# The first expert network in pairs of tiles, with four pairs in flight and a shorter inverse root

## The reference

```python
x = x + _L0_gnn_ref(_layernorm(x), ...)   # per relation sums of edges, block-diagonal weights
x = x + _L0_ffn_ref(_layernorm(x)[None], ...)[0]   # the part that the change touches
x = x + _L1_gnn_ref(_layernorm(x), ...)   # attention over edges
x = x + _L1_ffn_ref(_layernorm(x)[None], ...)[0]   # eight gated networks per row
```

```python
h = jax.nn.gelu(jnp.einsum('nd,edf->enf', xf, W1) + b1[:, None, :], approximate=False)
y = jnp.einsum('enf,efd->end', h, W2) + b2[:, None, :]
out = jnp.einsum('ne,end->nd', w_dense, y).reshape(B, S, D)
out = _layer_norm(out + x, gamma, beta)
```

## Time and profile before

| | |
|---|---|
| runs shown | 4926.8, 4935.69, 4936.24 us, median 4935.69 us |
| profiled execution | 4932.26 us, span 4930.4 us |
| mean granted TensorE clock | 0.842 of full speed |
| busy, share of the span | PE 84%, weight loads 66%, DVE 41%, ACT 18%, POOL 63% |
| `ffn0`, first hidden matmul to the end of the last row | 2176.84 to 2697.30 us |

### The profile page before, as it was taken

One profiled execution on the slowest core, in us unless ns is written; L12 is line 12 of the kernel. 1 busy time (PEld: TensorE's weight loads), 2 busy tenths in 40 slices (PEclk: granted clock), 3 DMA queues, 4 the chain that ended last, 5 costly groups with the idle time before them and its releaser, 6 DMA issues. The chain is left out here.

```text
span 4930.4 us, 66111 instructions
## 1 busy us (share of the span) xinstructions
PE 4146.8 (84%) x18994; PEld 3241.6 (66%) x18994; DVE 2022.2 (41%) x8072; ACT 895.6 (18%) x1880; POOL 3130.4 (63%) x3273
## 2 busy tenths in 40 slices
PE   2888878877788778858886689999999999999998
PEld 2777777877778778745564346666666666666665
DVE  5455555555555555524443223323332333233321
ACT  3111111111111111123332011111111111111112
POOL 3777777777777777710000677777777777777750
PEclk6667677777766776679997689999999999999999
DMA  5344444444444444411111544444444444444430
GB/s 166 113 122 121 122 122 121 121 122 123 121 121 121 121 121 123 121 56 40 46 39 33 157 118 118 123 126 123 118 123 127 122 118 127 128 123 117 127 94 10
DMA packets 270659, 544.10 MB, mean 110 GB/s; under 512 B 62129, under 2 KB 165825, under 8 KB 270482
## 3 DMA queue, kind: packets, MB, share of 16 engines
q0 software_dynamic: 155584, 431.06, 31.7%
q1 hardware_dynamic: 71890, 70.98, 4.6%
q10 hardware_dynamic: 43008, 40.36, 2.5%
HBM read 482.17 MB, written 59.99 MB: 110 GB/s over the span
## 5 line engine op out<-in xcount | busy, mean ns | idle before, releaser
L1560 POOL DMA_INDIRECT ring<-table,index x1616 | 1553.2, 961 | 548.6 <-issue 491.9
L651 POOL DMA_INDIRECT ring<-xn,index x1612 | 1528.9, 948 | 565.1 <-issue 477.3
L766 PE MATMUL bank<-spare,ring 128*128 128x64 f32 x6448 | 1063.7, 337 | 426.0 <-DMA ring<-xn,index 392.2
L766 PEld LDWEIGHTS bank<-spare,ring 128*128 128x128 f32 x6448 | 1027.2, 251 | 452.9 <-issue 398.8
L1731 PE MATMUL bank<-ring,acc 128*128 128x264 f32 x3232 | 884.4, 411 | 118.2 <-DMA ring<-table,index 112.1
L1731 PEld LDWEIGHTS bank<-ring,acc 128*128 128x128 f32 x3232 | 599.6, 196 | 424.5 <-DMA ring<-table,index 241.3
L1909 DVE TENSOR_SCALAR acc<-iota,off 128x128 f32<-128x128 f32 x1734 | 355.6, 298 | 636.3 <-ACT off L1573 633.3
L865 DVE TENSOR_TENSOR cells<-cells,bank 128x128 f32 x812 | 233.9, 288 | 427.5 <-PE bank L766 345.2
L845 DVE TENSOR_SCALAR spare<-iota,scal 128x64 f32<-128x64 f32 x1612 | 407.2, 337 | 0.0
L1747 PE MATMUL bank<-acc,wa 128*128 (+1 forms) x832 | 381.4, 601 | 26.7 <-ACT ework L1608 26.7
L1772 PE MATMUL bank<-wo,ework 128*128 128x256 f32 x1664 | 381.6, 383 | 1.8 <-DVE y L1980 1.8
(11 more groups left out here) (268 smaller groups left out, 3281.3 us busy)
## 6 DMA issues: line engine op xcount, KB each, us to landing
ring<-table,index POOLq DMA_INDIRECT x1616, 2.8
ring<-xn,index POOLq DMA_INDIRECT x1612, 2.8
sums<-acc ACTq DMA_DIRECT2D x101, 132.0 KB, 2.0
sums<-spare ACTq DMA_DIRECT2D x101, 128.0 KB
acc<-sums ACTq DMA_DIRECT2D x13, 528.0 KB
y<-x SPq DMA_DIRECT2D x13, 512.0 KB
table<-frow SPq DMA_DIRECT2D x48, 132.0 KB, 1.7
nsums<-sums ACTq DMA_DIRECT2D x49, 128.0 KB
```

Of the source, the lines that this page charges most:

```text
L651: pool.indirect_dma_start(ring[:, m * BT + t, :], None, k.xn_d, bass.IndirectOffsetOnAxis(ap=index[m][:, t:t + 1], axis=0)).then_inc(got[m ...
L766: ins = pe.matmul(win[q][:, t, h * CELLS:(h + 1) * CELLS], ring[:, m * BT + q * QUAD + t, h * P:(h + 1) * P], onehot[:, q * QUAD + t, :], ...
L1560: pool.indirect_dma_start(ring[:, par * BT + t, :], None, k.table1_d, bass.IndirectOffsetOnAxis(ap=index[par][:, t:t + 1], axis=0)).then_i ...
```

## The change

`ffn0` is written anew. The unit is a pair of tiles: 25 pairs, the last with one tile of 128 rows. `pair_steps` runs step s on every engine, and in step s there is work of four pairs: the hidden layer of pair s, the output of pair s-1 (both chunk by chunk, in turn), the norms and the turn of pair s-2, and the projection and the rows of pair s-3. There are four banks for the hidden chunks in place of two. PE's identity matmuls, ACT's `xg` and ACT's copy of y go away; in their place POOL makes `res`, x1 times its inverse deviation plus b2 (two instructions), beside the one that adds beta, and DVE adds `res` as it reads the bank (`add`). `gnn0` keeps the inverse deviations with one more DVE copy per tile. `inverse_root` is 11 instructions in place of 14. The first hidden matmul no longer waits for the load of `wp`.

```diff
@@ -160,13 +160,12 @@
     st.then(dve.tensor_scalar(t.bitcast(I32), x.bitcast(I32), 1, None, ALU.arith_shift_right))
     st.then(dve.tensor_scalar(guess.bitcast(I32), t.bitcast(I32), -1.0, float(0x5f3759df), ALU.mult, ALU.add))
     for _ in range(3):
-        st.then(dve.tensor_tensor(t, guess, guess, ALU.mult))
+        st.then(dve.scalar_tensor_tensor(t, guess, -0.5, guess, ALU.mult, ALU.mult))
         st.then(dve.tensor_tensor(t, t, x, ALU.mult))
-        st.then(dve.tensor_scalar(t, t, -0.5, 1.5, ALU.mult, ALU.add))
-        st.then(dve.tensor_tensor(guess, guess, t, ALU.mult))
-INVERSE_ROOT_STEPS = 14
+        st.then(dve.scalar_tensor_tensor(guess, t, 1.5, guess, ALU.add, ALU.mult))
+INVERSE_ROOT_STEPS = 11
 
 
 def past_waits(eng, k):
@@ -865,7 +864,7 @@
                     dve.tensor_tensor(here, here, win[q][:, u, :].rearrange("p (c n) -> p c n", n=NEAR), ALU.add
                                       ).then_inc(added if u == QUAD - 1 else chain, 1)
 
-            NORMS = 5 + INVERSE_ROOT_STEPS
+            NORMS = 6 + INVERSE_ROOT_STEPS
 
             def norm(j, par, loaded):
                 st = Steps(dve, steps, NORMS * j, k)
@@ -880,6 +879,7 @@
                 st.then(dve.bn_aggr(mv[:], stats[:]))
                 st.then(dve.tensor_scalar(var[:], mv[:, 1:2], LN_EPS, None, ALU.add))
                 inverse_root(dve, st, var[:], rstd[:], tmp[:])
+                st.done(dve.tensor_copy(k.rstd1[:, cols(j, 1)], rstd[:]))
                 if not (isinstance(j, int) and j == 0):
...
+def group_norm_steps(n):
+    return 2 * n + 1 + INVERSE_ROOT_STEPS
+PAIR = 2
+PCOLS = PAIR * P
+PAIRS = -(-NODE_TILES // PAIR)
...
+def pair_steps(eng, step):
+    first, last = 4, PAIRS - 3
+    assert first % 2 == 0 and last % 2 == 0
+    for s in range(first):
+        step(s, s % 2, s // 2)
+    with eng.Fori(first // 2, last // 2) as i:
+        step(2 * i, 0, i)
+        step(2 * i + 1, 1, i)
+    for s in range(last, PAIRS + 3):
+        step(s, s % 2, s // 2)
...
+    BANKS = 4
...
+        hid = a.sb("hid", [P, 2, C, PCOLS])
+        x1, res, x1b, x2 = (a.sb(f"f{n}", [P, 2, PAIR, D]) for n in ("x1", "res", "x1b", "x2"))
+        y, xn2 = (a.sb(f"f{n}", [P, PAIR, D]) for n in ("y", "xn2"))
...
+            def load(i, par):
+                if not (isinstance(i, int) and i < 2):
+                    sp.wait_ge(x1b_made, i - 1)
+                sp.dma_start(x1[:, par, 0:tiles_of_pair(i), :], rows_of(k.x1_all, 0, i)).then_inc(x_load[par], 16)
+            def store_x2(i, par):
+                sp.wait_ge(x2_done, i + 1)
+                sp.dma_start(rows_of(k.x2_all, AHEAD - AHEAD0, i), x2[:, par, 0:tiles_of_pair(i), :]
+                             ).then_inc(x2_stored[par], 16)
+            def store_row(i, t):
+                sp.wait_ge(row_done, PAIR * i + t + 1)
+                skip = AHEAD0 if isinstance(i, int) and i == 0 and t == 0 else 0
+                sp.dma_start(k.table1_d[cols(PCOLS * i + P * t + skip - AHEAD0, P - skip), :], row[skip:P, t, :]
+                             ).then_inc(row_stored[t], 16)
+            def step(s, par, half):
+                if is_pair(s + 1):
+                    load(s + 1, 1 - par)
+                if is_pair(s - 2):
+                    store_x2(s - 2, par)
+                if is_pair(s - 3):
+                    for t in range(tiles_of_pair(s - 3)):
+                        store_row(s - 3, t)
+            load(0, 0)
+            sp.dma_start(wp[:, :, 0:D], g["L1_gnn_W"].rearrange("(h p) d -> p h d", p=P)).then_inc(w_load, 16)
+            pair_steps(sp, step)
+            for par in range(2):
+                sp.wait_ge(x2_stored[par], 16 * len(range(par, PAIRS, 2)))
...
+            def residual(i, par, half):
+                n = tiles_of_pair(i)
+                here = res[:, par, 0:n, :]
+                pool.wait_ge(x_load[par], 16 * half + 16)
+                if not (isinstance(i, int) and i < 2):
+                    pool.wait_ge(y_added, PAIR * i - PAIR)
+                pool.tensor_tensor(here, x1[:, par, 0:n, :], k.rstd1[:, cols(PAIR * i, n)].unsqueeze(2).broadcast_to(
+                    [P, n, D]), ALU.mult).then_inc(res_step, 1)
+                pool.wait_ge(res_step, i + 1)
+                pool.tensor_tensor(here, here, each(b2[:], n), ALU.add).then_inc(res_made, 1)
+            def add_beta(i, par):
+                n = tiles_of_pair(i)
+                if not (isinstance(i, int) and i < 2):
+                    pool.wait_ge(x2_done, i - 1)
+                pool.tensor_tensor(x1b[:, par, 0:n, :], x1[:, par, 0:n, :], each(beta[:], n), ALU.add
+                                   ).then_inc(x1b_made, 1)
+            def step(s, par, half):
+                if is_pair(s):
+                    residual(s, par, half)
+                if is_pair(s - 1):
+                    add_beta(s - 1, 1 - par)
+            pool.wait_ge(small, 32)
+            pool.wait_ge(b2_kept, 1)
...
-                for h in range(H):
-                    pe.matmul(yb[:r, h * P:(h + 1) * P], xg[:, h, t * P:t * P + r], k.ident[:],
-                              start=(h == 0), stop=False, skip_group_check=True)
...
+            def hidden(i, par, c):
+                n = P * tiles_of_pair(i)
+                if not (isinstance(i, int) and i == 0 and c < BANKS):
+                    pe.wait_ge(h_kept, C * i + c - BANKS + 1)
+                for h in range(H):
+                    ins = pe.matmul(h_ps[c % BANKS][:, :n], k.w1[:, c // (C // 2), h, c % (C // 2) * P:(c % (C // 2) + 1) * P],
+                                    k.acc[:, h, cols(PCOLS * i, n)], start=(h == 0), stop=(h == H - 1))
+                ins.then_inc(h_made, 1)
+            def output(i, par, u):
+                t, first = u // (C // PAIR), u % (C // PAIR) * PAIR
+                if t >= tiles_of_pair(i):
+                    return
+                if first == 0:
+                    if not (isinstance(i, int) and i == 0):
+                        pe.wait_ge(y_added, PAIR * i - PAIR + t + 1)
+                    if t == 0:
+                        pe.wait_ge(h_kept, C * i + C)
+                for c in range(first, first + PAIR):
+                    ins = pe.matmul(y_ps[t], hid[:, par, c, t * P:(t + 1) * P], k.w2[:, c // (C // 2), c % (C // 2), :],
+                                    start=(c == 0), stop=(c == C - 1))
+                if first == C - PAIR:
+                    ins.then_inc(y_made, 1)
+            def turn(i):
+                pe.wait_ge(normed, i + 1)
+                if not (isinstance(i, int) and i == 0):
+                    pe.wait_ge(t_kept, i)
+                for t in range(tiles_of_pair(i)):
+                    for h in range(H):
+                        ins = pe.transpose(t_ps[:, h * PAIR + t, :], xn2[:, t, h * P:(h + 1) * P], k.ident[:])
+                ins.then_inc(turned, 1)
+            def project(i, t):
+                if isinstance(i, int) and i == 0 and t == 0:
+                    pe.wait_ge(wp_made, 1)
+                    pe.wait_ge(b2_kept, 1)
+                if t == 0:
+                    pe.wait_ge(t_kept, i + 1)
+                if not (isinstance(i, int) and i == 0 and t == 0):
+                    pe.wait_ge(p_moved, PAIR * i + t)
+                for h in range(H):
+                    ins = pe.matmul(p_ps, xt[:, h, t, :], wp[:, h, :], start=(h == 0), stop=(h == H - 1))
+                ins.then_inc(p_made, 1)
+            def step(s, par, half):
                 for c in range(C):
+                    if is_pair(s):
+                        hidden(s, par, c)
+                    if is_pair(s - 1):
+                        output(s - 1, 1 - par, c)
+                    if is_pair(s - 3) and c in (1, 4) and c // 4 < tiles_of_pair(s - 3):
+                        project(s - 3, c // 4)
+                if is_pair(s - 2):
+                    turn(s - 2)
+            pe.matmul(p_ps[:, 0:D], k.ones[0:1, :], k.b2[0:1, :], start=True, stop=True).then_inc(b2_made, 1)
+            pair_steps(pe, step)
...
-                act.copy(y[:r, t, :], y_ps[t % 2][:r, 0:D]).then_inc(y_moved, 1)
...
+            def keep(i, par, c):
+                n = P * tiles_of_pair(i)
+                act.wait_ge(h_made, C * i + c + 1)
+                act.activation(hid[:, par, c, :n], h_ps[c % BANKS][:, :n], ACT.Gelu,
+                               bias=k.b1[:, c // (C // 2), c % (C // 2):c % (C // 2) + 1]).then_inc(h_kept, 1)
...
+            def grow(i, t):
+                act.wait_ge(p_made, PAIR * i + t + 1)
+                act.activation(grown[:, t, :], p_ps[:, D:ROW1], ACT.Exp, scale=k.fm[:, 0:1],
+                               bias=k.fm[:, 1:2]).then_inc(grown_made, 1)
+            def step(s, par, half):
+                for c in range(C):
+                    if is_pair(s):
+                        keep(s, par, c)
+                    if is_pair(s - 3) and c in (1, 4) and c // 4 < tiles_of_pair(s - 3):
+                        grow(s - 3, c // 4)
```

(17 more changed lines are left out.)

## The result

The changed kernel takes 4975.2 us (median of 4 runs, 4966.0 to 4985.5), the kernel before 4931.5 us (4 runs, 4926.8 to 4936.2). The ratio is 1.0092, with a 95% interval of 1.0073 to 1.0111: slower by 44 us. The forecast was 4908 us, range 4874 to 4940, with 0.75 on faster and 0.10 on slower. It was wrong in sign, and the time lies outside the range.

A forecast was written before the change was run, and what follows sets the result against it. The prediction took a loop of waits in `ffn0`, through PE's second projection and DVE's norms, as the bound: 18.7 + 1.0 + 0.1 = 19.8 us a step. With 24.0 us gained in all, 4908 us, range 4874 to 4940.

The forecast's parts named there:

- bare chain: The loop's turn in `ffn0` without surcharges, from second projection to second projection through PE and DVE: 18.7 us a step.
- POOL on DVE: Surcharge in `ffn0` for POOL's additions running beside DVE's norms: 0.1 us a step.
- clock, without POOL's meeting: Surcharge in `ffn0` for PE's low clock behind its wait at the second projection: 1.0 us a step, bounds 0 and 1.69.
- the forecast's own sign of being wrong: In `ffn0`: PE waiting for ACT, steps under 18 or over 21 us, or stages around moving over 5 us.
- PE's own work: In `ffn0`, PE needs 15.9 us for a pair: hidden layer, output, projections and transposes.
- The loop: In `ffn0`, DVE's norms and row hold up PE's second projection; PE waits some 2.8 us once a step.
- ACT hidden: In `ffn0`, ACT has 10.1 us of work in a 19.8 us step, table loads included, off the path.
- POOL's additions: Three in `ffn0`, 1.2 us each, at the norms' head; slowing of DVE bounded by 0 and 2.5 us, 0.1 taken.
- the turn to slower: Rival in `ffn0`: POOL slows the norms, 2.5 us a step, 4958 us; decides from 1.2 us more; chance 0.06.
- The rival drawn from the Trainium skill: In `ffn0`, POOL stretches nine instructions of the first root by 1.97: 1.4 us a step, 4935 us; chance 0.04.
- Start and tail: In `ffn0`, the loop's first second projection at 2220.4; from step 24's second projection to the last row's start 38.6 us.
- Small parts: Outside `ffn0`: -0.4 us in `gnn0`, and -1.5 us for two shorter roots before the first gather of `gnn1_ffn1`.

The follow-up runs named there:

- small POOL: The changed kernel with POOL's three additions in `ffn0` cut to one column of each tile; 4917.1 us.
- filled wait: The changed kernel with eight unused matmuls on constants ahead of PE's wait for `p_moved`, in a bank taken from the hidden layer; 4922.1 us.
- both edits: The changed kernel with POOL's additions cut to one column and four unused matmuls in PE's wait; 6293.3 us, 0.9915 of before, on a slower chip.
- two-bank version: The changed kernel with a PSUM bank for each of the two projections and three hidden-layer banks in place of four; 4824.8 us.
- e1_forms: The changed kernel with three single-input DVE instructions of the norms written as two-input ones on the same tiles; 4976.9 us.
- e6_two_more_additions: The changed kernel with two more POOL additions, results unused, ahead of the one for beta; 5002.7 us.
- chunk 6: The changed kernel with the second projection moved from PE's chunk 4 to chunk 6; 4856.6 us.
- beta first: The changed kernel with POOL's beta addition issued ahead of the residual; 4954.7 us.
- root in 14 steps: The changed kernel with the inverse root in 14 instructions, as in the kernel before; 5008.8 us.

## Why the prediction was wrong

The four steps 22.60 (the change), 19.65 (small POOL), 20.34 (filled wait) and 18.45 (both) take the turn apart:

| term of the step | forecast | measured | from |
|---|---|---|---|
| bare chain | 18.7 | 18.45 | both edits |
| POOL on DVE | 0.1 | 1.89 | 20.34 - 18.45 |
| clock, without POOL's meeting | 1.0 | 1.20 | 19.65 - 18.45 |
| clock, in the change | 1.0 | 2.26 | 22.60 - 20.34 |
| step | 19.8 | 22.60 | |

Of the 2.80 us that a step is longer than forecast, 1.79 are POOL's term and 1.26 the clock's, less 0.25 for the chain. Steps of over 21 us were the forecast's own sign of being wrong. The two kernels with a filled wait also have three banks for the hidden layer in place of four; in the two-bank version three banks cost nothing.

*What bounds the kernel, and PE's own work.* Right: 15.9 us forecast, 16.03 measured where PE never waits.

*The loop.* Right, in place and in size (its pieces add up to 18.8, not 18.7). The wait stands at the second projection, ended by DVE behind `p_moved`, in every step. Its pieces: from the second projection to the last add 6.37 us with the clock up (2348.33 to 2354.70 in the filled wait) beside 6.3; from that add to the statistics 0.61 beside 0.86; norms 10.2 without POOL (both edits) beside 10.3; root instructions every 0.196 us beside 0.20.

*ACT hidden.* Right: 10.23 us busy a step beside 10.1, no wait for Gelu, with four banks or three, and four table loads of 1.28 us in each step. The Trainium skill's advice on table loads (ScalarE: Activation LUTs, Table sets) would have weighed against the change for nothing here.

*POOL's additions: the step that failed.* I wrote: "the bounds are 0 and, stretched as `xn2` was (x 1.97), 2.5 us a step; I take 0.1, the row is of a 256-column instruction and most of these have two elements." It was 1.89. That is 1.8 more than forecast, and from 1.2 more I had put the turn to slower. The choice of 0.1 rested on size, as if the additions slowed a rate. They don't: a DVE instruction of these forms that meets one stands until it ends, however small it is. The traces of this study hold 403 such instructions in `ffn0` that took between 0.9 and 1.4 us; every one ends 0.015 to 0.029 us behind the end of one of POOL's. The row already held this. It is a sum of four instructions; one by one, in the trace of the kernel before, they are:

```profile
L1325 DVE TENSOR_SCALAR fxn<-fx,fmv,frstd x4: 403/408/2532, 2266.3 to 2269.4; 128x256 f32<-128x256 f32 x4
```

Three took 403 to 408 ns, and one 2532: it began at 2266.63 and ended at 2269.16, POOL's addition at 2269.01. It is so in all twelve groups of that stage: one instruction of `xn2` ends 0.14 to 0.16 us behind the addition. The factor, 1.96 by the row's own numbers and not 1.97, was the mean of three untouched instructions and one that waited out an addition. Read so, the price does not scale with DVE's work but with the number and length of additions that follow each other: two of 1.27 us met here, less the 0.17 that each instruction takes anyway, and less gaps: 2.0.

The rival drawn from the Trainium skill (chance 0.04, 4935 us) had the right place and the wrong instructions and price. It counted nine two-input steps of the root; in the change two TENSOR_SCALARs stand, L1087 ahead of the root and L160, its first step. By the Trainium skill, SBUF — State Buffer, Who interferes with whom, a DVE instruction with two SBUF inputs, or in a 2-port mode, "fully blocks" while GpSimd holds the shared pair, and others do not contend. The runs agree as far as they go: two-input forms stood (means of 645 and 600 ns in `e1_forms`, 1.11 and 1.19 us in `e6_two_more_additions`), statistics and aggregates did not. That the two TENSOR_SCALARs ran in a 2-port mode no run shows. The rival took the exposed set from the skill and the factor from the row; one standing instruction for each addition would have given 2.0 us a step, 1.9 more than taken, and 4908 + 21 x 1.9 = 4948 us.

*The clock: the second term that failed.* Without POOL's meeting it was 1.20 beside 1.0. That is in part luck: the wait was then 2.1 us and not the 2.8 of the forecast, and an estimate for 2.8, on a line between the prices at 2.1 and 3.2, is 1.7. The price depends on the wait, and POOL's 1.9 us lengthened the wait from 2.1 to 4.1 us, with 1.1 more of low clock behind it. I added the two as if they were apart. The price by length of the wait: none to be seen at 0.7 to 1.0 us (chunk 6), 1.2 at 2.1, 1.9 at 3.2 (beta first: 21.42 - 18.45 - 1.04 for the norms), 2.3 at 4.1, 2.2 at 5.3 (root in 14 steps: 23.76 - 18.45 - 1.89 - 1.22), 1.6 at 6.1.

*Start and tail.* 6.0 us late at the first second projection, 4.7 of it the stage's own start in this execution. The tail from the last second projection of a full pair to the last row took 38.9 us, 38.6 forecast; the terms that the forecast names for it add up to 38.2. So of the 65.2 us between forecast and trace at the last row, 21 x 2.80 = 58.8 are the step. *Small parts.* From the last row to the first gather it was 27.47 us before and is 23.71 now; 1.5 of the 3.8 were forecast for the two roots there, and the same 1.5 is what the change with 14 steps gives back (25.25). The other 2.3 lie on SyncE: from the store of the last row to the first load of the next stage it was 5.11 us (2697.48 to 2702.59) and is 2.86 (2740.66 to 2743.52), which the forecast did not have. The copy of `rstd1` in `gnn0` doesn't show.

So the change pays 89 us on top of a stage that would otherwise be shorter than before by 51 (526.2 to 475.4): POOL's meeting and the clock.

## What to carry to other kernels

A row that sums several instructions hides a stall: before a stretched group becomes a factor, ask for its minimum, median and maximum, and look for an instruction of another engine that ends just as the longest one does. Surcharges on a loop of waits aren't independent where one of them lengthens an idle time of PE: price the clock for the wait that the other terms leave. And when a new order ties two halves of a pipeline through a buffer, count its copies first: one more PSUM bank for the projection, taken where it wasn't missed, was worth 150 us, while a faster root was worth 31 on the loop and next to nothing off it.

## What the runs showed of the hardware that was not expected

- A 128x2 instruction of DVE takes 0.17 us alone and 1.08 to 1.26 us when it meets a 128x512 addition of POOL (1.27 us), in the forms TENSOR_SCALAR, SCALAR_TENSOR_TENSOR and TENSOR_TENSOR, one instruction for each addition. BATCH_NORM_STATS2 (0.42) and BATCH_NORM_AGGREGATE (0.17) beside the same additions keep their times.
- Sixteen useless matmul instructions in each wait of 4.2 us made the stage 49 us shorter and the kernel faster (1.0092 to 0.9973 of before). The granted clock in the steps went from 0.87 to 1.00, and DVE's norms did not change.
- Behind a wait of 6.1 us the low clock cost less (23.96 - 18.45 - 1.89 - 2.0 = 1.6 us) than behind one of 4.1 (2.26) or 5.3 (2.2). Why stays open.
